# Setup of a two-layer AdaLN transformer kernel: fewer modulation rows first, lists and second modulation in the next block

## The reference, cut to what matters

```
mod = (silu(c) @ wmod).reshape(16, 6, 1, 256)        # c: 16x256, wmod: 256x1536
sa, ca, ga, sb, cb, gb = mod[:, 0] ... mod[:, 5]
ga = (2 * (ga >= 0) - 1) * maximum(abs(ga), 0.25)    # gb likewise
h = layernorm(x) * (1 + ca) + sa
x = x + ga * attention_part(h)      # layer 0: local attention, + bias bo, layernorm(gamma, beta), MLP, + b2
h = layernorm(x) * (1 + cb) + sb
x = x + gb * ffn_part(h)            # layer 0: sort 1024 tokens by expert, 8 experts, + bias
```

## Time and profile before

| | us |
|---|---|
| median of 3 runs | 3192.86 (3179.95 to 3193.56) |
| the profiled execution, its own time | 3183.52 |
| its span on the core | 3181.8 |

### The profile page before, as it was taken

One profiled execution on the slowest core, in us unless ns is written; L12 is line 12 of the kernel. 1 busy time (PEld: TensorE's weight loads), 2 busy tenths in 40 slices (PEclk: granted clock), 3 DMA queues, 4 the chain that ended last, 5 costly groups with the idle time before them and its releaser, 6 DMA issues. The chain is left out here.

```text
span 3181.8 us, 58120 instructions
## 1 busy us (share of the span) xinstructions
PE 3018.6 (95%) x19338; PEld 1850.6 (58%) x19338; DVE 2186.8 (69%) x6717; ACT 1562.6 (49%) x3529; POOL 1213.6 (38%) x1530
## 2 busy tenths in 40 slices
PE   7899999999998998899999999999999968999997
PEld 3566766666665674344444444444444327888886
DVE  6777777777763333678888888888888842445545
ACT  3566556565552113466666666666666631111111
POOL 3123232232234212234444444444443242455544
PEclk8899999999999999899999999999999989999998
DMA  8111010110122981222222222222222217999995
GB/s 292 7 53 45 33 64 33 33 64 33 35 100 79 315 297 52 71 58 68 73 74 74 75 71 73 73 77 78 78 78 73 80 35 213 242 272 280 272 263 173
DMA packets 291041, 354.70 MB, mean 111 GB/s; under 512 B 49855, under 2 KB 240562, under 8 KB 290752
## 3 DMA queue, kind: packets, MB, share of 16 engines
q1 hardware_dynamic: 261760, 313.28, 31.2%
q0 software_dynamic: 28464, 34.71, 5.0%
q10 hardware_dynamic: 544, 3.15, 0.3%
HBM read 234.02 MB, written 122.34 MB: 112 GB/s over the span
## 5 line engine op out<-in xcount | busy, mean ns | idle before, releaser
L2907 DVE TENSOR_REDUCE negmax<-psum 128x1 f32<-128x512 f32 x1024 | 670.7, 685 | 129.7 <-PE psum L3487 125.1
L2520 ACT ACTIVATE pT<-psum 128x512 f32<-128x512 f32 x1024 | 576.8, 600 | 258.8 <-PE psum L3513 225.4
L3487 PE MATMUL psum<-k_stack,q_stack 96*128 96x512 bf16 x1024 | 357.0, 388 | 17.4 <-DVE negmax L2907 10.3
L3513 PE MATMUL psum<-q_stack,k_stack 99*128 99x512 bf16 x1024 | 347.8, 382 | 8.1 <-ACT pT L2520 6.2
L4149 POOL DMA_INDIRECT src_rows<-ye,place x142 | 221.9, 1563 | 283.3 <-DVE ye L4208 251.7
L990 ACT ACTIVATE probs<-probs,negmax 128x256 f32<-128x256 f32 x512 | 252.8, 495 | 119.0 <-DVE negmax L1081 117.4
L4166 ACT ACTIVATE actT_x<-psum 128x512 f32<-128x512 f32 x142 | 84.8, 597 | 441.4 <-PE psum L4323 441.4
L3527 PE MATMUL psum<-pT,v_tile 128*32 128x512 f32 x2048 | 273.3, 606 | 1.6 <-ACT pT L2520 1.0
L4323 PE MATMUL psum<-xT_x,w_x 128*128 128x256 f32 x1136 | 260.3, 383 | 1.1 <-DMA w_x<-in_L_ffn_w_dram 1.1
L4335 PE MATMUL psum<-w_x,actT_x 128*128 128x256 f32 x1136 | 256.6, 379 | 0.0
L1081 DVE CUSTOM_DVE_ANT_0 probs<-psum,band_mask 128x256 f32<-128x256 f32 x512 | 181.6, 421 | 104.8 <-PE psum L1339 104.7
(11 more groups left out here) (420 smaller groups left out, 5602.8 us busy)
## 6 DMA issues: line engine op xcount, KB each, us to landing
w_x<-in_L_ffn_w_dram SPq DMA_DIRECT2D x142, 512.0 KB, 5.4
w_e<-in_L_ffn_w_dram SPq DMA_DIRECT2D x46, 1024.0 KB, 6.4
q_stacks<-q_part SPq DMA_DIRECT2D x192, 128.0 KB
q_stack<-q_stacks SPq DMA_DIRECT2D x64, 384.0 KB, 3.7
padded<-w_e SPq DMA_DIRECT2D x32, 650.0 KB, 6.0
xe<-padded SPq DMA_DIRECT2D x71, 260.0 KB, 5.2
gate_rows<-mods SPq DMA_DIRECT2D x66, 256.0 KB, 5.6
src_e<-src_rows SPq DMA_DIRECT2D x30, 512.0 KB, 6.5
```

What stands on the lines that cost most here:

```text
L2520: act.activation(pT[:, 4 * (s % 2) + r, :], bank(m, 2 + n % 2), ACT.Exp, scale=float(DHQ) ** -0.5)\
L2907: dve.tensor_reduce(negmax[:, p // REP, h:h + 1], bank(m, max_bank(b, 16 * g + p)), AX.X, ALU.max, negate=True).then_inc(max_read, 1)
L3487: pe.matmul(bank(m, max_bank(b, 16 * g + p)), q_stack[0:K_SCORE, h, t * P:(t + 1) * P], k_stack[0:K_SCORE, g, :], start=True, stop=True).t ...
L3513: pe.matmul(bank(m, 2 + n % 2), k_stack[:, g, kc * P:(kc + 1) * P], q_stack[:, REP * g + r, :], start=True, stop=True).then_inc(sT_done, 1)
```

## The change

Setup computes only layer 0's modulation and stores only rows 4 and 5 (those that GpSimd's first hidden rows read). The setup tiles that live on (second layer's weights, rows, biases, lists) are placed in the part of `m.x` that holds batches 7 to 15, whose loads wait until they are free (`LATE`). What moves into `local_attention_block`:

- TensorE: the second layer's modulation in three groups of four matmuls, one ahead of the first projection and two between projections, and the count of hits.
- VectorE: the hit list, ahead of the norm of batch 1.
- ScalarE: reading the second modulation and the counts, ahead of `body(0)`.
- GpSimd: the other seven rows of layer 0 (`first_rows`), behind the first hidden rows.
- SyncE: the store of those rows behind the norm rows of batch 1; gate rows of batch 0 and all further loads of x come behind that store. In setup the small weights come behind the attention weights and a bias row, then x of batch 1 and the second layer's weights; the bias rows and the routing lists come last, after the store.

GpSimd's constants start with the identity. Only two of the four sets of columns are made.

The core of the diff:

```diff
+    m.wmod1 = room(C * 6 * D).rearrange("p (c n) -> p c n", c=C)
...
         @block.sync
             for layer in (0, 1):
                 sp.dma_start(cond[:, layer, :], I[f"L{layer}_c"]).then_inc(cond_in, 16)
-            load_batch(0)
-            sp.dma_start(route_i...); sp.dma_start(m.route_w0...)
-            for i, n in enumerate(("L0_attn_b2", "L0_ffn_bias", "L0_attn_beta", "L0_attn_bo", "L0_attn_gamma")): ...
+            load_x(sp, m, I, 0, m.x_first)
             load_attention_weights(sp, m, I)
-            load_batch(1)
+            sp.dma_start(m.bias0[:, 3, :], I["L0_attn_bo"].partition_broadcast(B)).then_inc(bo_in, 16)
+            load_small_weights(sp, m, I)
+            load_x(sp, m, I, 1, m.x_second)
+            sp.dma_start(m.wmod1[:, :, :], I["L1_wmod"].rearrange("(c p) n -> p c n", p=P)).then_inc(m.x_second, 16)
+            sp.wait_ge(rows_ready, 2)
+            sp.dma_start(mods_dram[0, :, 4:6, :], m.rows0[:, 4:6, :]).then_inc(m.rows_out, 16)
+            for i, n in ((0, "L0_attn_b2"), (1, "L0_ffn_bias"), (2, "L0_attn_beta"), (4, "L0_attn_gamma")):
+                sp.dma_start(m.bias0[:, i, :], I[n].partition_broadcast(B)).then_inc(m.bias1_in, 16)
             for i, n in enumerate(("L1_attn_bo", "L1_ffn_ob")):
                 sp.dma_start(m.bias1[:, i, :], I[n].partition_broadcast(B)).then_inc(m.bias1_in, 16)
-            sp.wait_ge(rows_ready, 8)
-            sp.dma_start(mods_dram[0, :, :, :], rows[:, :, :]).then_inc(m.rows_out, 16)
+            load_routing(sp, m, I)
...
+            pool.wait_ge(bo_in, 16)
+            pool.wait_ge(mod_read, 1)
+            pool.tensor_tensor(m.rows0[:, 5, :], m.mod0[:, 0, :], m.bias0[:, 3, :], ALU.add).then_inc(rows_ready, 1)
+            pool.tensor_scalar(m.rows0[:, 4, :], m.mod0[:, 1, :], 1.0, None, ALU.add).then_inc(rows_ready, 1)
...
         @block.vector
             first_norm0(dve, m, 0)
+            dve.wait_ge(mod_read, 1)
+            dve.tensor_scalar(m.sign0[:, 0, :], m.mod0[:, 1, :], 1.0, None, ALU.add).then_inc(scale_ready, 1)
             dve.wait_ge(cols_done, 1)
...
         @block.tensor
-            pe.wait_ge(constants, 5)
+            pe.wait_ge(constants, 2)
...
+# local_attention_block, SyncE
             load_norm_rows(0)
+            load_mlp_weights(sp, m, I)
+            load_norm_rows(1)
+            sp.wait_ge(rows0_ready, 4)
+            sp.dma_start(mods_dram[0, :, 0:4, :], m.rows0[:, 0:4, :]).then_inc(m.rows_out, 16)
+            sp.dma_start(mods_dram[0, :, 6:9, :], m.rows0[:, 6:9, :]).then_inc(m.rows_out, 16)
+            sp.wait_ge(m.rows_out, 48)
             load_gate_rows(0)
-            load_mlp_weights(sp, m, I)
+            sp.wait_ge(m.x_third, 32)
             for b in (2, 3):
                 load_x(sp, m, I, b, m.x_third)
-            load_norm_rows(1)
             for b in range(4, B):
+                if b == LATE:
+                    sp.wait_ge(mod1_done, 3)
+                    sp.wait_ge(rank_done, 1)
                 load_x(sp, m, I, b, m.x_rest)
...
+            def first_rows():
+                mod, sign, rows, bias = m.mod0, m.sign0, m.rows0, m.bias0
+                gates = mod[:, 2:6:3, :]
+                step = Steps(pool, rows0_s, 0, 0)
+                step(pool.tensor_scalar(sign[:, :, :], gates, 0.0, 0.5, ALU.is_ge, ALU.subtract))
+                pool.wait_ge(m.bias1_in, 16 * 6)
+                step(pool.tensor_tensor(bias[:, 0, :], bias[:, 0, :], bias[:, 2, :], ALU.add))
+                step.settle()
+                step(pool.tensor_tensor(gates, gates, sign[:, :, :], ALU.mult))
+                pool.tensor_scalar(rows[:, 7, :], mod[:, 4, :], 1.0, None, ALU.add).then_inc(rows0_ready, 1)
+                step.settle()
+                step(pool.tensor_scalar(gates, gates, 0.125, 4.0, ALU.max, ALU.mult))
+                pool.tensor_copy(rows[:, 8, :], mod[:, 3, :]).then_inc(rows0_ready, 1)
+                step.settle()
+                step(pool.tensor_tensor(rows[:, 0:3:2, :], gates, sign[:, :, :], ALU.mult))
+                step.settle()
+                step(pool.tensor_tensor(rows[:, 3, :], rows[:, 2, :], bias[:, 1, :], ALU.mult))
+                step(pool.tensor_tensor(rows[:, 1, :], rows[:, 0, :], bias[:, 0, :], ALU.mult))
+                step.settle()
+                step(pool.tensor_tensor(sign[:, 0, :], rows[:, 3, :], m.later0.to_broadcast([B, D]), ALU.mult))
+                pool.tensor_tensor(rows[:, 6, :], rows[:, 0, :], bias[:, 4, :], ALU.mult).then_inc(rows0_ready, 1)
+                step.settle()
+                pool.tensor_tensor(rows[:, 1, :], rows[:, 1, :], sign[:, 0, :], ALU.add).then_inc(rows0_ready, 1)
...
             hidden_rows(0, 0)
+            first_rows()
...
+# TensorE
+            pe.wait_ge(m.x_second, 32)
+            second_modulation(0)
             pe.wait_ge(hT_act, 1)
             pe.wait_ge(hT_dve, 1)
             project_inputs(m.wq0, 0, 0, 7, q_done)
             project_inputs(m.wq0, 1, 0, 5, q_done)
             project_inputs(m.wk0, 0, 0, 6, k_done)
+            second_modulation(1)
             pe.wait_ge(q_ready, 1)
             project_inputs(m.wk0, 1, 0, 7, k_done)
+            second_modulation(2)
             pe.wait_ge(q_ready, 2)
             project_values(0, 0, 5)
+            count_experts()
             pe.wait_ge(k_ready, 1)
             project_values(1, 0, 6)
+            pe.wait_ge(mod1_read, 3)
+            pe.wait_ge(ranks_read, 3)
             body(0, 0, first=True)
...
+# VectorE, ahead of the norm of batch 1
+            dve.wait_ge(m.x_third, 32)
+            place(dve.tensor_copy(m.token0[:, :], m.token_i0[:, :]))
+            place(dve.tensor_copy(m.route_f[:, :], m.route_i[:, :]))
+            place(dve.tensor_copy(m.iota_f0, m.iota_i0[:, :]))
+            place.settle()
+            dve.tensor_tensor(m.hit0, ..., ALU.is_equal).then_inc(hit_ready, 1)
+            dve.wait_ge(m.x_second, 32)
             first_norm0(dve, m, 1, first_keys_values)
+            dve.wait_ge(ranks_read, 3)
             body(0, 0, first=True)
```

More of the change, by code:

```diff
@@ L472, in _ @@
-            dve.tensor_copy(rows[:, 8, :], mod[:, 3, :]).then_inc(rows_ready, 1)
-            step.settle()
-            dve.wait_ge(rows_ready, 6)
-            dve.scalar_tensor_tensor(out=rows[:, 1, :], in0=rows[:, 3, :], scalar=later[:, 0:1], in1=rows[:, 1, :],
-                                     op0=ALU.mult, op1=ALU.add).then_inc(rows_ready, 2)
+            dve.wait_ge(mod_read, 1)
+            dve.tensor_scalar(m.sign0[:, 0, :], m.mod0[:, 1, :], 1.0, None, ALU.add).then_inc(scale_ready, 1)
@@ L574 @@
 LOCAL_LOADS = 10
+LATE = 7
 MIXER_LOADS = 13 + 4 * C
@@ L1547, in body, with second_modulation, count_experts @@
                     down(1, spare(25))
+            def second_modulation(n):
+                for c in range(C):
+                    mm = pe.matmul(bank(m, 2 + n)[0:B, :], m.condT[:, 1, c, :], m.wmod1[:, c, 512 * n:512 * (n + 1)],
+                                   start=(c == 0), stop=(c == C - 1))
+                mm.then_inc(mod1_done, 1)
+            def count_experts():
+                pe.wait_ge(hit_ready, 1)
+                hits = m.hit0.rearrange("p j e -> p (j e)")
+                pe.matmul(bank(m, 0)[:, 0:NSORT * E], m.before0[:, :], hits, start=True, stop=True)
+                pe.matmul(bank(m, 0)[:, NSORT * E:2 * NSORT * E], m.ones0[:, :], hits, start=True, stop=True)\
+                    .then_inc(rank_done, 1)
+            pe.wait_ge(m.x_second, 32)
+            second_modulation(0)
             pe.wait_ge(hT_act, 1)
```

210 lines of the change are left out of this document (96 added, 114 removed).

## The result

The changed kernel took 3192.11 us (median of 20 runs, 3184.56 to 3201.27), the kernel before, run beside it, 3185.23 (20 runs, 3177.49 to 3193.75): ratio 1.0019, 95% interval 1.001 to 1.0028. The forecast was 3184 and a gain of 3.8 us; the change loses 6 us (0.0019 x 3185). The median lies inside the range of 3171 to 3196, but the sign is wrong. A second comparison gave 1.0023 (1.0011 to 1.0034).

The account below looks back on a forecast made before the run. The expert stage ends last, behind a serial prefix. Setup gains 8.5 us; added matmuls, counting and VectorE/GpSimd interference leave 4.1 at the row maximum, less 0.3: -3.8 from the mean 3187.5 gives 3184, range 3171 to 3196.

Parts of the forecast that it names:

- a serial prefix: Everything before the expert stage: time taken out ahead of the first scores leaves the end too, unless something gives it back.
- rival C: Setup: SyncE stalls at the routing lists, setup ends 9.3 us later; 5.5 us slower, 3193; chance 0.11.
- Setup: Setup block without the second modulation lot: attention entry at 20.7 against 29.2, gain 8.5 us.
- B: Head: routing lists take 10 us to land, delaying VectorE's second norm; gain 1.8, time 3186; chance 0.13.
- The covered matmuls: Head: first four added matmuls take 2.2 us in the 2.1 us wait for hidden tiles, so cost nothing.
- the sum: Head: first row maximum at 41.2 against 45.3, 4.1 us; 0.3 off for expert counting; -3.8 us.
- The collision: End of head: VectorE's four normalising instructions beside GpSimd's row work; 1.0 us on the path, between 0 and 2.
- The port rule: End of head: each normalising step could wait out a 0.72 us GpSimd instruction; 2.9 us, not 1.0.
- Rival D: Second layer's rows land late for ScalarE's second batch; each microsecond past 97.6 is lost; 3188; chance 0.03.
- The chances: Whole kernel: faster 0.08, same 0.87, slower 0.05; 0.5% (16 us) taken as what a measurement can tell.

Follow-up runs that it names:

- the two head experiments: Changed kernel plus 15 VectorE increments, second modulation's weights loaded by ScalarE: 0.9991; also GpSimd's remaining rows behind batch 1's hidden rows, x 2-6 before their store: 1.0007.

## Why the prediction was wrong

**The step that failed** is the first: that everything is a serial prefix, so that "a microsecond taken out ahead of the first scores is taken out of the end unless something later gives it back", with nothing later named but transfers. The order of work is serial, and 0.65 us of the head's gain did reach 878 us. But the edit also took 15 instructions off VectorE's list, and that moves the edges of the blocks in which all its later code is loaded. In one place a load that had cost 1.12 us came to cost 4.10, with TensorE's slow restart behind it, and as much again is lost behind attention, by placement too as far as the shifts show. With the shift undone ahead of the loop the same edit gives 0.9993 and 0.9991, 2.2 and 2.9 us faster, where the forecast was 3.8 and the head's trace says 1.5; both intervals reach 1.0 (0.9983 to 1.0002, 0.9982 to 1.0), so even that gain is just at the edge of what the runs can tell. The moved work was judged right in direction and too well in size, and about 9 us of placement were not judged at all. No rival held it. That 3192 lies inside the range is luck: the range was drawn for the scatter of executions and for rival C, which had the right time by a mechanism (a stall of SyncE) that did not occur.

The Trainium skill, Runtime: NRT & Kernel Launch, "Instruction fetch mechanics", says that an engine's instructions come in 16 KiB blocks while it executes, that crossing an edge is mostly hidden, and that a taken branch breaks the sequential prefetch. The trace fits the mechanism and differs on the numbers: 8 KB in each packet of queue 14, a period of 128 instructions, and 3.7 to 4.1 us in the open for the first block loaded behind a loop. That the loop is what left the block unloaded fits the packets (none from 340 to 865 us), but was not tried.

**Setup** was right: entry at 20.2 (20.7). Rival C (stall at the lists) and B (late lists: they held VectorE 1.3 us, off the path) did not happen.

**The covered matmuls** were mis-sized. "2.2 for 2.1, so nothing" left out that their weights, issued at 12.24 behind all other loads of setup, land only near 22.2. The four also took 3.25 us, not 2.2, at a granted clock of 0.50 (a third of the 7.02 would have been 2.34, and that lot ran partly at the higher clock). They cost until 25.5 where 22.9 was forecast. The projections behind them ran 0.6 us faster than the sum had it, since the granted clock rose under the covered group (0.50 over 22 to 24 us, 0.74 over 24 to 26), so the scores came 2.0 us late.

**The collision**: 1.0 us taken, 1.64 measured, 2.26 with the load on ScalarE's queue, and none with GpSimd idle. The port rule of the Trainium skill (SBUF — State Buffer, "Who interferes with whom"), worked out in the prediction, gave 2.9; the measured values lie between, and its direction is confirmed by the two head experiments. Together 2.0 + 0.65 = 2.6 us is the difference between 41.2 and 43.8. Behind it the sum took only 0.3 us more off, while some 2 us of lead were gone at 96 us and 0.6 at 112; which wait takes them was not traced.

**Rival D** was rightly put aside for this kernel (the second layer's rows, forecast to land near 88 and in any case before 90, landed near 93, the columns were issued from 93.10, and ScalarE was not held), and the kernel that moved the rows 14 us back showed that it is real: 16.45 us of wait, for the stores' landing, where 8.41 for VectorE stood.

**The chances.** What a measurement can tell was set at 0.5% by the scatter of single executions; medians of a dozen runs and more told 0.1%. The forecast gave no chance to an effect of the compiled list, which is as large as the whole of what the head could give.

## What to carry to other kernels

An edit that adds or removes instructions moves all later code of that engine; before an effect of 0.3% is put down to the edit, shift the list back with idle instructions, and by a whole block, and look for waits put down to "issue" at the first block loaded behind a loop, with an instruction packet inside them. The label alone proves nothing: at the router (L3044, 2577.75 us) VectorE stood 16.23 us for "issue" in one profile of the kernel with 15 increments ahead of the loop, not at all in the other, and the first was the faster execution (3176.09 against 3177.82). Where such a wait stands on the path, move its edge by some instructions into a place where the engine has work queued. And read a queue as a list: here a small store behind a 1.5 MB load landed with the load (8.0 us, and 3.6 with the load on another queue), and a wait for "all stores landed" belongs where the stores have long been over.

## What the runs showed of the hardware

- VectorE stood idle 3.66 to 4.10 us for a block of 8 KB of instructions in six kernels, at the same instruction for shifts of 0 and 128 and (in the kernel before) 113, even where the DMA engines were 5% busy over the last 1.5 us of it. It vanished for shifts of 8, 15 and 64. The packet of 8 KB stands some 1.8 us ahead of the instruction that waited, in all of them.
- Behind such a wait, in which TensorE had 2.0 to 2.4 us without work, eight matmuls took 5.40 us instead of 3.60 in five kernels (granted clock 0.50 over 882 to 884 us in the changed one) and 3.70 in a sixth, at a clock of 1.00.
- Increments of a semaphore are not free in number: 113 and 128 of them put VectorE's first instruction at 11.80 and 13.18 us instead of 7.6 and 7.4; 64 left it at 7.7. In the kernel before the head became shorter all the same, since TensorE's matmuls then stood closer together and ran at the higher clock.
- Four VectorE normalising instructions of 128x256 took 1.37 us alone and 2.7 to 3.6 us beside GpSimd's row instructions of 16 partitions.
- Left open: which waits make up the 4.5 us behind the attention block, and why the kernel before does not have them with 113 increments; why the granted clock of the same head differs between executions; why the kernels with zero stores taken forward gained more than the 3 to 4 us that the trace accounts for.
